# Gathering the routed rows as float32r high and low parts in place of fp32 products

## What is computed

```python
x = x + tanh(g_xattn[0]) * xattn(layernorm(x), ctx, ...)
g = layernorm(x).reshape(b, s // 32, 32, 512)          # groups of 32 tokens
logits = einsum('bntd,des->bntes', g, Wc) + bc + tie   # 128 experts
perm = (logits == max(logits, axis=-3)).astype(f32)    # one-hot over the 32 tokens
permuted = einsum('bntd,bntes->bnesd', g, perm)        # the gather
inner = relu(einsum('bnesd,esdf->bnesf', permuted, W1) + b1)
out = einsum('bnesf,esdf->bnesd', inner, W2) + b2
x = x + tanh(g_ffn[0]) * einsum('bnesd,bntes->bntd', out, perm)
```

## Time and profile before

| | |
|---|---|
| median of three runs | 1735.38 us (1732.0 to 1741.31) |
| the profiled execution | 1737.52 us, its span 1735.6 us |
| attention, up to the first gather | 880.8 us |
| expert stage, first gather of batch 0 to last gather of batch 15 | 795.2 us |
| tail | 59.6 us |
| mean granted clock of TensorE | 0.987 |

### The profile page before, as it was taken

The page is one execution under the profiler, slowest core; times in us unless marked ns, Lnnn a source line. Parts: engine busy times, 40 slices in busy tenths (PEclk is TensorE's granted clock), DMA queues, the critical chain, the costliest instruction groups (busy, mean ns, idle before and its releaser), DMA issues.

```text
span 1735.6 us, 51613 instructions
## 1 busy us (share of the span) xinstructions
PE 1605.5 (93%) x22424; PEld 1126.5 (65%) x22424; DVE 1298.3 (75%) x1893; ACT 739.4 (43%) x966; POOL 861.4 (50%) x1020
## 2 busy tenths in 40 slices
PE   8899999999999999999888998999998889898994
PEld 4677777777777777777676554666555566555662
DVE  5777777777777777777748776778777777776766
ACT  3632323233323333332234555555555455555552
POOL 3468777877787788778641233122233122233122
PEclk9999999999999999999999999999999999999998
DMA  7634545545454455545565888778888787887875
GB/s 290 176 101 151 178 141 174 165 150 164 162 187 138 164 164 163 154 158 170 164 217 174 217 218 223 213 221 202 231 222 220 211 223 191 202 229 210 225 183 153
DMA packets 180593, 325.31 MB, mean 187 GB/s; under 512 B 23056, under 2 KB 33168, under 8 KB 178960
## 3 DMA queue, kind: packets, MB, share of 16 engines
q1 hardware_dynamic: 135104, 239.15, 42.9%
q0 software_dynamic: 17616, 32.52, 11.8%
q10 hardware_dynamic: 27648, 50.34, 8.8%
HBM read 243.23 MB, written 78.71 MB: 185 GB/s over the span
## 4 chain that ended last, share of the span: by engine, by line
PE 61%; DVE 14%; DMA 12%; issue 6%; ACT 3%; POOL 2%; SPq 1%; ACTq 0%; POOLq 0%; DVEq 0%
PE ps L1493 11%; PE ps L951 11%; PE ps L998 10%; PE ps L1463 7%; PE ps L1011 5%; DMA xin<-out 5%; PE ps L1517 3%; PE ps L966 3%; PE ps L1532 3%; DMA out<-xin 3%; PE ps L1024 3%; DMA sel<-lg_scratch 2%; DVE mx L730 2%; DVE res L1405 2%; PE ps L985 2%
## 5 line engine op out<-in xcount | busy, mean ns | idle before, releaser
L184 POOL TENSOR_SCALAR xin<-xin,r_all,nb_all 128x512 f32<-128x512 f32 x128 | 113.7, 891 | 507.3 <-DMA xin<-out 379.5
L1389 DVE STREAM_TRANSPOSE res<-res 128x2048 f32<-128x2048 f32 x128 | 292.0, 2295 | 0.1
L1341 ACT ACTIVATE gat<-ps 128x1536 f32<-128x1536 f32 (+1 forms) x128 | 170.7, 1345 | 204.8 <-PE ps L1463 204.8
L951 PE MATMUL ps<-xTh,qh 128*128 128x512 f32 x512 | 210.3, 411 | 5.6 <-DVE qs L747 2.0
L951 PE MATMUL ps<-xTh,ql 128*128 128x512 f32 x512 | 201.1, 393 | 0.0
L951 PE MATMUL ps<-xTl,qh 128*128 128x512 f32 x512 | 200.5, 392 | 0.0
L1405 DVE COPY res<-ps 128x1024 f32<-128x1024 f32 x128 | 156.7, 1224 | 58.1 <-PE ps L1517 58.0
L1463 PE MATMUL ps<-sel,xin 32*128 32x128 f32 x4096 | 153.7, 285 | 36.6 <-ACT sel L215 10.3
L1312 POOL DMA_DIRECT2D out<-xin x120 | 119.9, 1124 | 97.3 <-DVE xin L1228 85.6
L552 POOL TENSOR_TENSOR xTl<-xT,xTh 128x512 fp32r<-128x512 f32 x128 | 160.5, 1283 | 12.0 <-ACT xTh L616 12.0
L1351 ACT ACTIVATE res<-ps 128x1024 f32<-128x1024 f32 x128 | 131.1, 1025 | 78.4 <-PE ps L1517 78.4
(11 more groups left out here) (169 smaller groups left out, 3288.5 us busy)
## 6 DMA issues: line engine op xcount, KB each, us to landing
gat<-in_W ACTq DMA_DIRECT2D x192, 256.0 KB, 5.6
xT<-in_xT SPq DMA_DIRECT2D x32, 1024.0 KB, 6.1
xin<-in_x SPq DMA_DIRECT2D x64, 512.0 KB, 3.8
out<-xin SPq DMA_DIRECT2D x64, 512.0 KB, 4.0
xin<-out SPq DMA_DIRECT2D x128, 256.0 KB, 4.2
xin<-in_W SPq DMA_DIRECT2D x128, 256.0 KB, 4.0
out<-xin POOLq DMA_DIRECT2D x120, 256.0 KB, 7.3
xT<-in_W SPq DMA_DIRECT2D x68, 256.0 KB, 4.5
```

Of the source, the lines that this page charges most:

```text
L184: e.tensor_scalar(self.xn[:, t, :], self.xn[:, t, :], self.r[:, i, t:t + 1], self.nb[:, i, t:t + 1], ALU.mult, ALU.add).then_inc(self.m_xn ...
L951: last = e.matmul(ps[:, 2 + n % 2, :], a[:, c, n * DH:(n + 1) * DH], b[:, c, :], start=(k == 0), stop=(k == len(parts) - 1))
L1341: e.activation(o, v, ACT.Copy).then_inc(m_gaA.sem, 1)
L1389: e.transpose(v, v).then_inc(m_tr.sem, 1)
```

## The change

The normed rows are split into a float32r high part (ScalarE, one 128x(4x128) piece at a time, into the new two-slot buffer `xhigh`) and the rest (GpSimd, written in place over the piece of `xn`, under the name `xlow`: `xlow` and `selr` are declared and released at once, so `xin` and `sel` are laid over the same bytes). Each product of a gather becomes two float32r products that accumulate, one of `xhigh`, one of `xlow`, both against `selr`. On ScalarE high part n+2 follows copy n; the high parts 0 and 1 of batch i+1 stand after `rest(i, 3)` and `rest(i, 5)`. On GpSimd low parts 2 to 7 open a batch and low parts 0 and 1 of the next close it. To make room the DMA scratch goes from 2048 to 1024, and in the attention part a few loads share semaphores.

```diff
+        with nc.sbuf_tensor("xlow", [P, NT, D], F32R) as xlow:
+            pass
         xin = sb0("xin", [P, RING, TH, D])
...
+        with nc.sbuf_tensor("selr", [P, NT, E], F32R) as selr:
+            pass
         sel = sb("sel", [P, NT, E])
+        xhigh = sb("xhigh", [P, 2, TH, P], F32R)
...
+        def rows_of(i, n):
+            return xn[:, n % 2 * TH:(n % 2 + 1) * TH, piece(i, n) // 2 * P:(piece(i, n) // 2 + 1) * P]
...
@@ def gpsimd(e)
+            def low(i, n):
+                e.wait_ge(m_xh.sem, m_xh.at(i, n))
+                c, h = piece(i, n) // 2, n % 2
+                e.tensor_tensor(xlow[:, h * TH:(h + 1) * TH, c * P:(c + 1) * P], rows_of(i, n), xhigh[:, n % 2].bitcast(F32),
+                                ALU.subtract).then_inc(m_xl.sem, 1)
+            low(0, 0)
+            low(0, 1)
             for i in range(B):
+                for n in range(2, 2 * C):
+                    low(i, n)
...
+                if live(i + 1):
+                    low(i + 1, 0)
+                    low(i + 1, 1)
...
@@ def scalar(e)
+            def high(i, n):
+                if n < 2:
+                    e.wait_ge(m_xn.sem, m_xn.at(i, n * TH + TH - 1))
+                if n >= 2:
+                    e.wait_ge(m_gap.sem, m_gap.at(i, n - 2))
+                elif i:
+                    e.wait_ge(m_gap.sem, m_gap.at(i - 1, 2 * C - 2 + n))
+                e.activation(xhigh[:, n % 2], rows_of(i, n), ACT.Copy).then_inc(m_xh.sem, 1)
...
+                    if i == 0:
+                        high(0, 0)
+                        high(0, 1)
                     for n in range(2 * C):
                         copy(i, n)
+                        if n + 2 < 2 * C:
+                            high(i, n + 2)
...
                 for u in range(8):
                     if live(i):
                         rest(i, u)
+                    if u in (3, 5) and live(i + 1):
+                        high(i + 1, (u - 3) // 2)
...
@@ def gather(i, n)
                 if n < 2:
                     e.wait_ge(m_sel.sem, m_sel.at(i, h))
-                    e.wait_ge(m_xn.sem, m_xn.at(i, h * TH + TH - 1))
+                e.wait_ge(m_xl.sem, m_xl.at(i, n))
                 for t in range(TH):
-                    for g in range(GT):
-                        r = slice(g * G, (g + 1) * G)
-                        last = e.matmul(ps[:, front(n) + g, t * E:(t + 1) * E], xn[r, h * TH + t, c * P:(c + 1) * P], sel[r, h * TH + t, :],
-                                        start=True, stop=True)
+                    for k, v in enumerate((xhigh[:, n % 2], xlow[:, h * TH:(h + 1) * TH, c * P:(c + 1) * P])):
+                        for g in range(GT):
+                            r = slice(g * G, (g + 1) * G)
+                            last = e.matmul(ps[:, front(n) + g, t * E:(t + 1) * E], v[r, t, :], selr[r, h * TH + t, :],
+                                            start=(k == 0), stop=(k == 1))
...
-            e.wait_ge(d_const.sem, d_const.at(0, 2))
+            e.wait_ge(d_const.sem, d_const.at(0, 5))
...
-    nc = bacc.Bacc("TRN2", target_bir_lowering=False, num_devices=1, dynamic_dma_scratch_size=2048)
+    nc = bacc.Bacc("TRN2", target_bir_lowering=False, num_devices=1, dynamic_dma_scratch_size=1024)
```

More of the change, by code:

```diff
@@ L111, in build @@
                          ident_in, cos_in, sin_in, b1, b2, kr_dram, vc_dram, out)
-        ffn = experts(nc, top, ps, kept, d_kept, consts, gate_f, xin, ring, d_ring, route, m_b2s, m_row, logits_landed, W1, W2, out)
+        ffn = experts(nc, top, ps, kept, d_kept, consts, gate_f, xin, xlow, ring, d_ring, route, m_b2s, m_row, logits_landed, W1, W2, out)
         with nc.Block() as blk:
@@ L167, in __init__, with lay @@
         self.m_sT, self.m_sel = mark("sT", 2), mark("sel", 2)
-        self.selT = self.sel = self.room = None
-    def lay(self, sel, selT, room):
-        self.sel, self.selT, self.room = sel, selT, room
+        self.selT = self.selr = self.room = None
+    def lay(self, selr, selT, room):
+        self.selr, self.selT, self.room = selr, selT, room
     def load(self, e, i, t):
@@ L214, in chosen @@
         e.wait_ge(self.m_sT.sem, self.m_sT.at(i, h))
-        e.activation(self.sel[:, h * TH:(h + 1) * TH, :].rearrange("p t e -> p (t e)"), self.ps[:, h, :], ACT.Copy).then_inc(self.m_sel.sem, 1)
+        e.activation(self.selr[:, h * TH:(h + 1) * TH, :].rearrange("p t e -> p (t e)"), self.ps[:, h, :], ACT.Copy).then_inc(self.m_sel.sem, 1)
 def attention(nc, top, ps, ident, small, gate_x, gate_f, xin, xT, consts, const_loads, kept, kept_loads, d_kept,
@@ L315, in attention @@
         d_ctxT = [pmark(f"ctxT{c}", 2 if c == 1 else 1, 16) for c in range(C)]
-        d_rs, d_small, d_kvw, d_qw = pmark("rs", 1, 16), pmark("small", 5, 16), pmark("kvw", 1, 16), pmark("qw", 1, 16)
-        d_tab, d_ow, d_const = pmark("tab", 2, 16), pmark("ow", 1, 16), pmark("const", 3, 16)
+        d_small, d_kvw, d_qw = pmark("small", 5, 16), pmark("kvw", 2, 16), pmark("qw", 1, 16)
+        d_tab, d_ow, d_const = pmark("tab", 2, 16), pmark("ow", 1, 16), pmark("const", 6, 16)
         d_krs = pmark("krs", 6, 16)
@@ L338, in attention @@
         d_kb = [mark(f"kb{k}", unit=16) for k in range(2)]
-        d_bias = mark("bias", 3, 16)
         m_b2l = mark("b2l", 3)
@@ L386, in sync @@
         def sync(e):
-            e.dma_start(rs1[:], rms).then_inc(d_rs.sem, 16)
+            e.dma_start(rs1[:], rms).then_inc(d_kvw.sem, 16)
             e.dma_start(kvraw[:, 0], kv_w[:, 0]).then_inc(d_kvw.sem, 16)
@@ L410, in sync @@
                 e.dma_start(o[:], v).then_inc(d_const.sem, 16)
-            e.dma_start(bias_parts[0][0], b2_dram[:, 0:2]).then_inc(d_bias.sem, 16)
-            e.dma_start(bias_parts[1][0], b1_dram).then_inc(d_bias.sem, 16)
+            e.dma_start(bias_parts[0][0], b2_dram[:, 0:2]).then_inc(d_const.sem, 16)
+            e.dma_start(bias_parts[1][0], b1_dram).then_inc(d_const.sem, 16)
             e.wait_ge(m_kvs.sem, m_kvs.at(0, C - 1))
-            e.dma_start(bias_parts[2][0], b2_dram[:, 2:4]).then_inc(d_bias.sem, 16)
+            e.dma_start(bias_parts[2][0], b2_dram[:, 2:4]).then_inc(d_const.sem, 16)
             e.wait_ge(m_ksc.sem, m_ksc.at(0, 1))
@@ L674, in bias_first @@
                 w, o = bias_parts[k]
-                e.wait_ge(d_bias.sem, d_bias.at(0, 2))
                 e.activation(o, w, ACT.Copy).then_inc(m_b2h.sem, 1)
@@ L793, in values_lo @@
                 e.tensor_tensor(vTl[:, v], ps[:, 2 + h, :], vTh[:, v].bitcast(F32), ALU.subtract).then_inc(m_vTl.sem, 1)
-            e.wait_ge(d_rs.sem, d_rs.at(0))
+            e.wait_ge(d_kvw.sem, d_kvw.at(0, 1))
             e.tensor_scalar(rs1[:], rs1[:], 1.0, None, ALU.add).then_inc(m_sc1.sem, 1)
             e.wait_ge(m_sc1.sem, m_sc1.at(0))
-            e.wait_ge(d_kvw.sem, d_kvw.at(0))
             for c in range(C):
@@ L1121, in attention, with experts @@
         return Stage(sync, gpsimd, scalar, vector, tensor), logits_landed
-def experts(nc, top, ps, kept, d_kept, consts, gate_f, xin, ring, d_ring, route, m_b2s, m_row, logits_landed, w1_dram, w2_dram, out):
+def experts(nc, top, ps, kept, d_kept, consts, gate_f, xin, xlow, ring, d_ring, route, m_b2s, m_row, logits_landed, w1_dram, w2_dram, out):
     st = ExitStack()
@@ L1142, in experts @@
         hid = lambda i: spare(i)[:, 0:Q * NG].rearrange("p (q n) -> p q n", n=NG)
-        route.lay(sel, selT, lambda i, h: spare(i + 1)[:, Q * NG:2 * Q * NG] if h else sel[:].rearrange("p t e -> p (t e)"))
+        route.lay(selr, selT, lambda i, h: spare(i + 1)[:, Q * NG:2 * Q * NG] if h else sel[:].rearrange("p t e -> p (t e)"))
         y = xin[:, 3]
@@ L1156, in experts @@
         m_xn, m_sel = route.m_xn, route.m_sel
+        m_xh, m_xl = mark("xh", 2 * C), mark("xl", 2 * C)
         live = lambda i: 0 <= i < B
```

## The result

The changed kernel takes 1841.91 us (median of 4 runs, 1840.15 to 1845.62), the kernel before 1733.69 us measured beside it (4 runs). The ratio is 1.0623, 95% interval 1.0579 to 1.0667: 6.2% slower. The forecast was 1934 us, range 1838 to 1982. The time lies at the lower end of the range, 92 us under the forecast and 4 us from rival (a), which gave 1846 us. The direction was right, and the largest term of the sum was wrong by nearly its whole size.

A forecast was written before the change was run, and what follows sets the result against it. Inside a batch TensorE was taken as the bound; at batch changes the chain returning the next row tiles is as long. Terms 88 + 53 + 38 + 20 = +199 us on 1735.4 gave 1934 us, range 1838 to 1982.

The forecast's parts named there:

- rival (a): Gathers: weight loads hide behind streaming, a step of 0.054 us, gather term 0; 1846 us; chance 0.11.
- The gathers, +88: TensorE's gathers: twice the loads, not hidden, 0.11 us a step; +111 us, net +88 (0 to +122) after filled waits.
- rival (c): Gathers: a float32r row-strip product takes a quarter of the fp32 one, -57 us; 1789 us; chance 0.05.
- ScalarE's stop, +53: Batch change: ScalarE's high part 1 waits for row tile 7 (its end is X), holding rest and chosen; +53 us (13 x 4.1).
- The clock, +38: TensorE idles 4 to 7 us at 13 batch changes, then runs at the 1.2 GHz level; +2.9 us each, +38.
- Batch 0, +20: Expert stage start: low part 0 stands behind late_logits on GpSimd, gather 0 moves +21.2 us; net +20 us (16 to 24).
- The parts inside a batch, 0: ScalarE's and GpSimd's added work inside batches stays hidden; only piece 2 is late, 1 us in 3 batches, taken as 0.
- The constants and the scratch, 0: TensorE's wait for six constants instead of three, and the smaller DMA scratch for adding stores; taken as 0.
- rival (d): The smaller scratch fills and adding stores wait: 1934 + up to 98 us, some 1990 to 2030; chance 0.03.

The follow-up runs named there:

- a_stream64: Changed kernel, each gather product streaming only 64 of the 128 selection columns, loads still 128 wide; 1848.39 us, one execution.
- a_load64: Changed kernel, each gather product loading only 64 of the 128 weight columns, streaming all 128; 1823.39 us, one execution.
- b_wait: Kernel before, fp32 gathers and no split, plus one ScalarE wait behind rest(5) for row tile 7 of the next batch; 1770.34 us, ratio 1.0225.
- batch0: Changed kernel with the attention's last logits spread over GpSimd's queue between low parts 0 to 4; 1829.08 us, ratio 1.0529 to the kernel before.
- fp32_first_two: Changed kernel with pieces 0 and 1 of each batch, and all of batch 0, gathered by fp32 products; 1738.75 us, ratio 1.0031 to the kernel before.
- b_scratch: Kernel before with the DMA scratch at 1024 in place of 2048; 1728.23 us, ratio 0.9980.
- b_stream64: Kernel before, each fp32 gather product streaming only 64 of 128 columns; 1747.67 us, one execution, against 1737.23 us for the kernel before.
- all_moved: Changed kernel with high part 1 behind the chosen copies, low parts 0 and 1 earlier, last logits spread between low parts; 1776.47 us, ratio 1.0239 to the kernel before.

## Why the prediction was right, and where it was not

That the time lies in the range is luck in one part: the range reached down to a rival that set the term of the gathers to 0, and this term is 0 for a reason that neither the forecast nor the rival had.

**The gathers, +88: wrong, about 0.** The step that failed is the first sentence of that part, "Removed are 32 fp32 products per gather, added 64 float32r ones", and with it "So fp32 costs two passes, not more". I took the 32 records of a gather for 32 products; the code has 16, and L1047, read as sixteen products of 0.429 us, has 8 (two halves by four chunks), so that one takes 0.86 us where a float32r product takes 0.23. The page's 4096 records of L1463 over 128 gathers of 16 products would have shown it, and the changed kernel has the same 4096. The rest of the argument held: a set of four loads takes 0.11 us, the load of a float32r product is as long as that of an fp32 record, and it does not hide. With 32 loads before and 32 after, its result is 0: the piece takes 3.07 us after, 3.12 before. Rival (a) gave this number for another reason (loads that hide, a step of 0.054 us); the step of 0.11 us, and a_stream64 and a_load64, exclude that reason.

The Trainium skill's rule of four passes for true fp32 (FP8 and Floating Point Precision, TensorE Precision Notes), which the prediction held against the trace, says what the runs show: two records of two passes. The trace does agree with it, other than the prediction says. By it the streaming of a gather halves, as the prediction drew from it for rival (c); it does (16 products of four passes against 32 of one), and nothing is won, since the loads stay. For the loads the Trainium skill (TensorE: Matmul & The Clock Gate, LDWEIGHTS) gives columns divided by 1.2, in ns, which is 107 for 128 columns and 53 for 64, whatever the rows. The runs agree for loads of 32 rows, with 0.11 and 0.06 us.

**ScalarE's stop, +53: right in mechanism and in size where it stands.** Gather 0 at X + 3.6 (forecast 3.4), gather 1 at X + 5.3 (forecast 4.5; gather 0 takes 1.75 us at the low clock), in 14 changes of batch instead of 13: into batch 4 row tile 7 now ends 6.8 us behind `rest(3, 5)`, where it was level before. The +4.58 us per batch make 64 us. What the forecast lacked is the give-back that b_wait shows, 1.45 us per batch: alone, the stop and its clock cost 39.5 us.

**The clock, +38: the place right, the size unsettled.** The forecast had 6.8 us at the low level behind each pause. Of the changes into batches 2 to 15, b_wait has that at nine, and its gathers 1 to 7 are not even longer. The changed kernel has 13.7 us at eleven of them (one is 1179.00 to 1192.60 above), with pauses of the same length, and gather 1 to gather 7 grows by 1.73 us, 24 us in all, in which gather 2's wait for VectorE's copy (19.2 us, 1.4 each) has its part. Stop and clock together are 86 us against 91. That these two agree is partly chance: the forecast has neither the give-back nor the longer low clock. Of the 86 us b_wait accounts for 39.5; the rest comes only with the parts in the queues and in the gathers, and no run divides it further.

**Batch 0, +20: right.** 19.0 us, by the place in GpSimd's queue, and batch0 took back 12.8 us of the time by another order of the queue.

**The parts inside a batch, 0: right for pieces 3 to 7, too small for piece 2.** In the changed kernel gather 2 waits for VectorE's copy instead; with the waits of the batch change gone, gather 2 waits 1.9 us for its low part in 14 batches (fp32_first_two), not 1 us in 3.

**The constants and the scratch, 0: right in the time** (b_scratch for the scratch; the constants were not tried alone). But the smaller scratch did leave the sign that the prediction named for rival (d), gaps ahead of the adding stores. GpSimd's stores in the kernel before and in b_scratch (busy us, mean ns, idle before):

```profile
L1312 POOL DMA_DIRECT2D out<-xin x120 | 119.9, 1124 | 97.3 <-DVE xin L1228 85.6 <-DMA gat<-in_W 10.3 <-ACT xin L1230 1.2
...
L1312 POOL DMA_DIRECT2D out<-xin x120 | 108.8, 941 | 163.6 <-DVE xin L1228 87.7 <-issue 65.7 <-ACT xin L1230 6.1
```

The 65.7 us without a releaser cost nothing there.

**The sum.** By these readings 0 + 86 + 19 = 105 us, the difference of the spans; the medians differ by 108. Forecast 199 less the wrong 88 is 111. (The prediction starts its sum from 1737.5, 1736.5 and 1735.4 in turn; 1934 is 1735.4 + 199, and the upper end of its range, 1982, is 1737.5 + 245.)

What stays open: why the same pause is followed by 6.8 us of low clock with fp32 gathers and 13.7 with gathers by parts. The two stretches differ in how long the array streams beside its loads, and in gather 2's wait. No run changes one of them alone for fp32 gathers behind the stop. In the gathers by parts, half the stream (a_stream64) leaves 13.7 us or more at eleven of the 14 changes, half the load (a_load64) 6.8 to 17.1. Without the stop, b_stream64 bears on it. Its fp32 gathers stream half as long and nothing else is changed, and yet the granted clock of its expert stage is 0.95 against 0.99, with 75 us at the low level against 20. The run took 10 us longer than the kernel before; it is one execution, and so a hint and no proof:

```profile
881.40:1686.00 804.60, 724.49 (x17464) 481.67 (x17464) 590.22 (x494) 432.29 (x478) 198.19 (x242) 0.95 0.77 211
```

## What to carry to other kernels

Count the products in the code and divide the trace's records by them before a duration is given to one: an fp32 product here was two records with a load each. Replacing fp32 by float32r high and low parts saves streaming only. So it wins nothing at 128 columns against 128, where the loads are the bound, and should pay where the streamed operand is much wider than the loaded one; by the rows, an estimate, 0.86 us against 2 x 0.23 at 512 columns. And new work goes behind the instructions that others wait for: none of the 108 us was added TensorE work; they began in two in-order queues, where a waiting or a late instruction stood in front of others that were due, and the clock that fell behind the pauses is in them.

## What the runs showed of the hardware

A weight load of 128 columns took 0.11 us for four row strips together, in fp32 and in float32r alike. In float32r it took 0.06 us for 64 columns, and 0.21 us for 128 at the low clock. An fp32 product was two records of two passes: 0.86 us at 512 columns, against 0.23 for a float32r one. The low clock also came behind short pauses. In all_moved, at the change into batch 5, TensorE waited 0.82 us ahead of gather 0 and 1.33 us ahead of gather 1; the sets of four go from 0.11 to 0.21 us apart within gather 1:

```profile
1157.93 0.33 PE L1511 MATMUL ps<-selr,xhigh 32*128 32x128 f32 x4 [1.33 <-POOL xlow L1328]
...
1158.40 0.40 PE L1511 MATMUL ps<-selr,xhigh 32*128 32x128 f32 x4
1158.52 0.49 PE L1511 MATMUL ps<-selr,xlow 32*128 32x128 f32 x4
1158.73 0.49 PE L1511 MATMUL ps<-selr,xhigh 32*128 32x128 f32 x4
```

The adding stores took 6.2 us from issue to landing after, 7.3 before. The difference goes with the scratch and not with the longer stage: the ten profiles with a scratch of 1024 have 5.8 to 6.7 us, b_scratch 6.5, and the four with 2048 have 7.2 or 7.3, b_wait with its longer stage 7.3. That b_scratch would stay at 7.3 was expected and missed.
